# An expert loop rebuilt: biases from picked tables, second-layer weights in place, SiLU on ScalarE

## The reference

```python
xn = layernorm(x)
xm = xn * time_mix + shift(xn) * (1 - time_mix)
k = exp(min(xm @ Wk.T, 60)); v = xm @ Wv.T; r = xm @ Wr.T
# per channel, with a decay: wkv = sum_u W[t,u] k[u] v[u], sum_k = sum_u W[t,u] k[u] + 1e-16
s = (sigmoid(r) * wkv / sum_k) @ Wo.T
top1 = argmax(xn @ Wg + bg)                       # one of 8 experts for each token
y = relu(xn @ W1[top1] + b1[top1]) @ W2[top1] + b2[top1]      # 128 -> 512 -> 128
out = x + s * silu(y)
```

## Time and profile before

| | |
|---|---|
| median of 3 runs | 225.92 us |
| lowest of them | 225.53 us |
| the profiled execution's span | 224.6 us |
| PE busy | 193.5 us (86%) |
| DVE busy | 143.8 us (64%) |
| ACT busy | 123.2 us (55%) |
| POOL busy | 121.1 us (54%) |

### The profile page before, as it was taken

The page is one execution under the profiler, slowest core; times in us unless marked ns, Lnnn a source line. Parts: engine busy times, 40 slices in busy tenths (PEclk is TensorE's granted clock), DMA queues, the critical chain, the costliest instruction groups (busy, mean ns, idle before and its releaser), DMA issues.

```text
span 224.6 us, 4169 instructions
## 1 busy us (share of the span) xinstructions
PE 193.5 (86%) x1140; PEld 141.5 (63%) x1140; DVE 143.8 (64%) x335; ACT 123.2 (55%) x265; POOL 121.1 (54%) x196
## 2 busy tenths in 40 slices
PE   8829999995999999999999999999999999990000
PEld 3329996443447777787877877777777777770000
DVE  1599626799671278686876589666896668110792
ACT  2015555463489777767856578665787557640000
POOL 7055904472643576755875657755577556323250
PEclk9975555899799999999999999999999999997555
DMA  4939949200011111102111110111201122101994
GB/s 110 274 76 314 306 119 285 72 0 0 12 37 26 47 38 37 47 24 50 34 36 35 35 47 23 47 35 35 47 23 47 28 42 40 33 12 50 301 290 130
DMA packets 23818, 18.21 MB, mean 81 GB/s; under 512 B 3600, under 2 KB 20496, under 8 KB 23808
## 3 DMA queue, kind: packets, MB, share of 16 engines
q1 hardware_dynamic: 20560, 12.90, 20.2%
q0 software_dynamic: 2528, 5.18, 8.9%
q10 hardware_dynamic: 720, 0.01, 0.2%
HBM read 11.30 MB, written 6.75 MB: 80 GB/s over the span
## 4 chain that ended last, share of the span: by engine, by line
PE 75%; DVE 14%; DMA 6%; SPq 1%; issue 1%; DVEq 0%; ACT 0%; POOL 0%; POOLq 0%
PE ps L1001 20%; PE ps L1009 19%; PE ps L1000 11%; PE ps L921 6%; PE ps L952 4%; PE ps L1020 4%; PE ps L982 4%; PE ps L931 3%; DMA x_sb<-in_L_attn_x 3%; DVE ohlo L618 3%; DVE kT L759 3%; PE ps L1011 3%; DMA kT<-g_rows 2%; DVE stats L503 1%; DMA g_rows<-gout,si 1%; DVE kT L764 1%
## 5 line engine op out<-in xcount | busy, mean ns | idle before, releaser
L446 POOL DMA_INDIRECT g_rows<-gout,si x39 | 40.3, 1032 | 20.7 <-issue 13.9
L428 POOL DMA_INDIRECT xg<-xn_rows,gi x36 | 37.8, 1050 | 16.5 <-POOL si L436 9.0
L1009 PE MATMUL ps<-w2e,ohhi_hidif 128*128 128x128 f32 x312 | 45.2, 288 | 0.0
L650 DVE TENSOR_TENSOR gout<-ps,sgm 128x128 f32<-128x128 f32 x39 | 11.3, 289 | 50.3 <-ACT sgm L847 38.1
L1009 PEld LDWEIGHTS ps<-w2e,ohhi_hidif 128*128 128x128 f32 x312 | 37.7, 191 | 2.6
L841 ACT ACTIVATE ohhi_hidif<-ps 128x512 f32<-128x512 f32 x39 | 23.4, 599 | 29.1 <-remote 14.4
L1001 PE MATMUL ps<-xgT,w1e 128*128 128x128 f32 x156 | 38.1, 326 | 0.0
L1000 PE MATMUL ps<-xgT,w1e 128*128 128x128 f32 x156 | 30.2, 275 | 0.0
L1001 PEld LDWEIGHTS ps<-xgT,w1e 128*128 128x128 f32 x156 | 23.2, 188 | 6.7
L836 ACT COPY w2e<-w 128x512 f32 x39 | 24.1, 618 | 5.0 <-issue 4.7
L825 ACT COPY w1e<-w 128x512 f32 x39 | 24.1, 618 | 3.1 <-issue 0.5
(11 more groups left out here) (157 smaller groups left out, 304.6 us busy)
## 6 DMA issues: line engine op xcount, KB each, us to landing
x_sb<-in_L_attn_x SPq DMA_DIRECT2D x8, 256.0 KB, 6.9
w<-in_L_ffn_W SPq DMA_DIRECT2D x1, 2048.0 KB, 10.8
xn_rows<-xn_sb SPq DMA_DIRECT2D x2, 1024.0 KB, 6.7
kT<-g_rows SPq DMA_DIRECT2D x8, 256.0 KB, 5.0
out_x<-kT SPq DMA_DIRECT2D x8, 256.0 KB, 3.0
xg<-xn_rows,gi POOLq DMA_INDIRECT x40
g_rows<-gout,si POOLq DMA_INDIRECT x39, 2.3
wnat<-in_L_attn_Wk SPq DMA_DIRECT2D x1, 64.0 KB, 2.7
```

What stands on the lines that cost most here:

```text
L428: g.indirect_dma_start(xg[j][:, :], None, xn_rows, bass.IndirectOffsetOnAxis(gi[:, j:j + 1], 0)).then_inc(gathered[j], 16)
L446: g.indirect_dma_start(g_rows, bass.IndirectOffsetOnAxis(si[:, j:j + 1], 0), gout[j][:, :], None).then_inc(scattered[j], 16)
L1009: t.matmul(psYe[j % 2][:, 0:P], hidT[j % 2][:, cols], w2e[j % 2][:, cols], start=(c == 0), stop=False)
```

## The change

- **First-layer bias.** `b1` is loaded as 32 rows (expert, chunk) of 128, three times over, so that 96 rows hold the three bf16 parts (`bias_rows`). A table `pick1` holds, for each expert and chunk, 128 columns with ones in the three rows that belong to it. One matmul of 512 columns, at an address taken from a register, puts the whole bias into the PSUM bank, and the four weight products add to it. It replaces four bias products.
- **Second layer.** Its bias is one product of `ones` with `pick2`, at the register's address, and its weights are read in place in `w2`, at register addresses. The copy to `w2e` is gone. PE reads `etab` itself, once for each slot.
- **SiLU** is one operation of ACT, in place of the sigmoid there and a product on DVE. It waits for the scatter that frees `gout`.
- **The loop is written out** on every engine. POOL gathers and scatters with columns of `gidx` and `sidx`, not staged. PE waits before its first slot for all of k, v, r and for the tables.
- **The attention on DVE** stands by itself after the last block of k and v, no longer between the slots; `project` runs at slots 8, 12, ... 36 (`PROJECT_AFTER`, `PROJECT_EVERY`). The sigmoid of r is applied as r leaves PSUM, for all eight blocks on ACT. `kef` (exp(time_first) k + 1e-16) is computed on ACT for a whole batch behind each exp of k.
- **In the front**, POOL builds `same_row`, ACT copies it to `pick1` and computes the exponentials of the decays ahead of the first square root. The bias rows no longer go out of SBUF and back.

```diff
-        bias_nat = sb("bias_nat", [P, (E * HID + E * P) // P])
-        bias_r = sb("bias_r", [P, 2, (E * HID + E * P) // P])
-        bias_part = sb("bias_part", [P, 3, (E * HID + E * P) // P], BF16)
-        bias_mat = sb("bias_mat", [BR, HID + P], BF16)
+        bias_nat = sb("bias_nat", [BK, 2, P])
+        bias_r = sb("bias_r", [BK, 2, 2, P])
+        bias_part = sb("bias_part", [BK, 3, 2, P], BF16)
+        bias_rows = sb("bias_rows", [BK, 2, P], BF16)
+        same_row = sb("same_row", [P, BQ], BF16)
+        pick1 = sb("pick1", [BK, BQ, P], BF16)
+        pick2 = sb("pick2", [BK, E, P], BF16)
...
-            sp.dma_start(bias_nat[:, 0:E * HID // P],
-                         b1.rearrange("e h -> (e h)").rearrange("(p c) -> p c", p=P)).then_inc(ld_small, 16)
-            sp.dma_start(bias_nat[:, E * HID // P:],
-                         b2.rearrange("e h -> (e h)").rearrange("(p c) -> p c", p=P)).then_inc(ld_small, 16)
-            sp.wait_ge(ld_small, 16 * 7)
+            sp.wait_ge(bias_clear, 1)
+            for j in range(3):
+                sp.dma_start(bias_nat[j * BQ:(j + 1) * BQ, 0, :],
+                             b1.rearrange("e (c h) -> (e c) h", h=P)).then_inc(ld_bias, 16)
+                sp.dma_start(bias_nat[j * BQ:j * BQ + E, 1, :], b2).then_inc(ld_bias, 16)
+            sp.wait_ge(ld_small, 16 * 3)
             sp.wait_ge(ld_proj, 16 * 4)
+            sp.wait_ge(ld_bias, 16 * 6)
             sp.dma_start(w1[:, :, :], W1.rearrange("e d h -> d e h")).then_inc(ld_w1, 16)
             sp.dma_start(w2[:, :, :], W2.rearrange("e (c p) d -> p (e c) d", p=P)).then_inc(ld_w2, 16)
-
-            sp.wait_ge(bias_split, 1)
-            n1 = E * HID // P
-            for j in range(3):
-                rows = bias_mat[j * E:(j + 1) * E, :]
-                sp.dma_start(rows[:, 0:HID].rearrange("e (p c) -> e p c", c=n1),
-                             bias_part[:, j, 0:n1]).then_inc(bias_rows_in, 16)
-                sp.dma_start(rows[:, HID:].rearrange("e (p c) -> e p c", c=E),
-                             bias_part[:, j, n1:]).then_inc(bias_rows_in, 16)
...
+            step.link(g.memset(same_row[:, :], 0.0))
+            for m in range(0, P, BQ):
+                ins = g.affine_select(out=same_row[:, :], in_=same_row[:, :], compare_op=ALU.not_equal, fill=1.0,
+                                      base=-m, pattern=[[-1, BQ]], channel_multiplier=1)
+                if m + BQ < P:
+                    step.link(ins)
+            ins.then_inc(same_row_ready, 1)
+            g.memset(bias_nat[:, 1, :], 0.0).then_inc(bias_clear, 1)
...
+            for j in range(3):
+                rows = slice(j * BQ, (j + 1) * BQ)
+                ins = g.tensor_copy(bias_rows[rows, :, :], bias_part[rows, j, :, :])
+            step.link(ins)
+
+            g.tensor_tensor(pick2[:, :, :], bias_rows[:, 1, :].unsqueeze(1).to_broadcast([BK, E, P]),
+                            same_row[0:BK, 0:E].unsqueeze(2).to_broadcast([BK, E, P]), ALU.mult
+                            ).then_inc(bias_ready, 1)
...
+            def gather(s):
+
+                j = s % RING
+                if s >= RING:
+                    pool.wait_ge(xgT_ps, s - RING + 1)
...
+                                     bass.IndirectOffsetOnAxis(gidx[:, s:s + 1], 0)).then_inc(gathered[j], 16)
+
+            def scatter(s):
...
+            for s in range(RING):
+                gather(s)
+            pool.wait_ge(idx_ready, 1)
+            for s in range(SLOTS):
+                if s + RING < SLOTS:
+                    gather(s + RING)
+                if s >= 2:
+                    scatter(s - 2)
+            scatter(SLOTS - 2)
+            scatter(SLOTS - 1)
...
+                v.tensor_tensor(den[:, :], kef[:, here], zk[:, 0:BLK], ALU.add).then_inc(dve_step, 1)
...
-            gate_rows(TURNS - 1, LAST - 1, reused=True)
+            dve.wait_ge(kvr_out[2], NB)
+            for q in range(NB):
+                if q % NBB == 0:
+                    dve.wait_ge(k_ready, q // NBB + 1)
+                    dve.wait_ge(kef_ready, q // NBB + 1)
+                attend(q)
...
+            act.wait_ge(same_row_ready, 1)
+            s.copy(pick1[:, :, :], same_row[0:BK, :].unsqueeze(2).to_broadcast([BK, BQ, P])).then_inc(pick1_ready, 1)
...
+            act.wait_ge(ld_dec, 16 * 2)
+            s.activation(dec[:, :], tdec[:, :], ACT.Exp).then_inc(act_step, 1)
+            s.activation(ef[:, :], tfir[:, :], ACT.Exp).then_inc(act_step, 1)
+            act.wait_ge(act_step, 1)
+            s.activation(a_exp[:, :], dec[:, :], ACT.Exp, scale=-1.0).then_inc(dec_ready, 1)
             deviation(0)
...
+                act.wait_ge(kvr_ps[2], k + 1)
+                s.activation(rT[:, here], psY[:, :], ACT.Sigmoid).then_inc(kvr_out[2], 1)
...
+            for k in range(ACT_BLOCKS, NB):
+                act.wait_ge(kvr_ps[2], k + 1)
+                s.activation(rT[:, k * BLK:(k + 1) * BLK], psY[:, :], ACT.Sigmoid).then_inc(kvr_out[2], 1)
+
             def exp_k(b):
+                here = slice(b * T, (b + 1) * T)
                 act.wait_ge(k_capped, b + 1)
-                s.activation(kT[:, b * T:(b + 1) * T], kT[:, b * T:(b + 1) * T], ACT.Exp).then_inc(k_ready, 1)
+                s.activation(kT[:, here], kT[:, here], ACT.Exp).then_inc(k_ready, 1)
+                act.wait_ge(act_step, 2)
+                act.wait_ge(k_ready, b + 1)
+                s.activation(kef[:, here], kT[:, here], ACT.Copy, bias=K_EPS, scale=ef[:, 0:1]
+                             ).then_inc(kef_ready, 1)
...
+            def silu_y(n):
+
+                act.wait_ge(y_ps, n + 1)
+                if n >= RING:
+                    act.wait_ge(scattered[n % RING], 16 * (n // RING))
+                s.activation(gout[n % RING][:, :], psYe[n % 2][:, 0:P], ACT.Silu).then_inc(g_ready, 1)
...
+            copy_w1(0)
+            copy_w1(1)
             exp_k(0)
-            copy_w1(0, 1)
-            act.wait_ge(ld_w2, 16)
-            copy_w2(0, 0)
-            copy_xgT(0, 0)
+            copy_xgT(0)
             exp_k(1)
             act.wait_ge(inv_ps, 1)
-            turn(0, first=True)
-            act.wait_ge(kvr_out[2], NB)
             act.wait_ge(xn_stored, 16 * BATCH)
-            turn(1, attends=True)
-            with act.Fori(2, TURNS - 1) as i:
-                turn(i, attends=True, projects=True)
-            turn(TURNS - 1, last=True, projects=True)
-            sigmoid_y(TURNS - 1, LAST - 1)
+            for n in range(SLOTS):
+                if n + 1 < SLOTS:
+                    copy_xgT(n + 1)
+                relu(n)
+                if n + 2 < SLOTS:
+                    copy_w1(n + 2)
+                q, r = divmod(n - PROJECT_AFTER, PROJECT_EVERY)
+                if n >= PROJECT_AFTER and r == 1 and q < NB:
+                    copy_s(q)
+                if n:
+                    silu_y(n - 1)
+            silu_y(SLOTS - 1)
...
+            def layer1(n, e):
+
+                t.matmul(psH[n % 2][:, :], bias_rows[:, 0, :],
+                         pick1[:, bass.ds(e * HC, HC), :].rearrange("p c d -> p (c d)"), start=True, stop=False)
+                pe.wait_ge(layer1_in, n + 1)
+                pe.wait_ge(w1e_in, n + 1)
...
                     cols = slice(c * P, (c + 1) * P)
-                    weights = (w1e[j % 2][:, cols], xgT[j % 2][:, :])
-                    bias = (bias_mat[:, cols], sel_t[j][:, :])
-
-                    one, two = (bias, weights) if c % 2 == 0 else (weights, bias)
-                    t.matmul(psH[j % 2][:, cols], *one, start=True, stop=False)
-                    last = t.matmul(psH[j % 2][:, cols], *two, start=False, stop=True)
+                    last = t.matmul(psH[n % 2][:, cols], w1e[n % 2][:, cols], xgT[n % 2][:, :],
+                                    start=False, stop=c == HC - 1)
                 last.then_inc(hid_ps, 1)
...
+            def layer2(n, e):
+
+                if n >= 2:
+                    pe.wait_ge(g_ready, n - 1)
+                t.matmul(psYe[n % 2][:, 0:P], ones[0:BK, :],
+                         pick2[:, bass.ds(e, 1), :].rearrange("p o d -> p (o d)"), start=True, stop=False)
+                pe.wait_ge(hid_ready, n + 1)
                 for c in range(HC):
                     cols = slice(c * P, (c + 1) * P)
-                    t.matmul(psYe[j % 2][:, 0:P], hidT[j % 2][:, cols], w2e[j % 2][:, cols],
-                             start=(c == 0), stop=False)
-                t.matmul(psYe[j % 2][:, 0:P], sel_t[j][:, :], bias_mat[:, HID:],
-                         start=False, stop=True).then_inc(y_ps, 1)
+                    last = t.matmul(psYe[n % 2][:, 0:P], hidT[n % 2][:, cols],
+                                    w2[:, bass.ds(e * HC + c, 1), :].rearrange("p o d -> p (o d)"),
+                                    start=False, stop=c == HC - 1)
+                last.then_inc(y_ps, 1)
...
+            def expert(n):
+
+                return pe.value_load(etab[0:1, n:n + 1], min_val=0, max_val=E - 1)
```

(22 more changed lines are left out.)

342 lines of the change are left out of this document (80 added, 262 removed).

## The result

| | before | after |
|---|---|---|
| median, times beside each other | 226.34 us | 208.38 us (208.01 to 209.28) |
| ratio of the times | 1 | 0.9226, 95% interval [0.9188, 0.9264] |
| span of the profiled execution | 224.6 us | 206.6 us |
| PE busy | 193.5 us | 159.3 us |

The ratio compares fast runs alone: one of the four runs behind the 226.34 took 289.62 us and is not in it. Timed again, the changed kernel gave the same (0.9246 [0.919, 0.9301]); a third time it gave 0.9821 [0.9777, 0.9865], which the last experiments are about.

The account below looks back on a forecast made before the run. PE's slot beat was taken as the bound: 77.2 entry + (134.4 - 20.5) loop + 2.7 half clock = 193.8, plus a 22.2 tail = span 216.0; median 1.3 above, 217.3 us. Range: 211 less a little to 229.

Parts of the forecast that it names:

- the entry: Way into the expert loop: ACT's work after PE's last k, v, r product puts layer 1 of slot 1 at 77.2.
- the half clock: First stretch of the loop: PE at half clock until about 82.5, costing 2.7 us more, bounds nothing and 6.
- rival 2: Slot loop: POOL becomes the beat, held up by DVE; 3.2 against 3.0 us a slot, 8 more, 225; chance 0.13.
- the terms of the loop on PE: Slot on PE: layer 1 1.41, layer 2 1.15, transpose 0.21; 2.77 us, 0.54 less, 20.5 us over 38 slots.
- the port rule: POOL beside DVE: two-input or two-port DVE operations would shut POOL out and stretch it past PE's beat; forecast set it aside.
- Rival 1: PE between layer 2 and next transpose: register work not hidden, up to 1.0 us a slot, 256 us; chance 0.17.
- The tables in the r loop: ACT's r loop: a Sigmoid table load each turn, 1.28 us where PE has slack, counted as 0 to 0.7.
- The front: Before k, v, r: decays' exponentials precede ACT's first square root, which comes 0.65 us late, all passed on to PE.
- rival 4: Slot loop: PE's clock never comes back up; half clock throughout, some 110 us more, 325; chance 0.04.
- The tail: Behind PE's end: 22.5 us loses the gate product, 0.30, leaving 22.2.
- the eight projections: Projections on PE within the loop: each keeps its eight passes, 0.99 us at most, with no gain counted.

Follow-up runs that it names:

- the last experiments: Changed kernel unaltered, beside one without DVE's attention: 222.58 us, ratio 0.9821; changed kernel with turns 2 to 8 of ACT's slots looped again: 225.28 us.
- the flat kernel: Changed kernel with ACT's loop over the first six blocks of k, v, r written out: 203.08 us, ratio 0.8988; repeated, 203.34 us.
- again_tanh: Changed kernel with ACT's k, v, r loop written out, key scaling moved to DVE and the gate from a tanh; unaltered repeat: 198.89 us, ratio 0.8834.

## Why the prediction missed

**What bounds it: right for the kernel before, half right for the changed one.** PE's beat was the bound, the loop gains, the entry and the half clock take some back. But from about 103 us on it is POOL that sets the beat (rival 2). Direction and order of size held; the time was 9 us too high.

**The failed step: the terms of the loop on PE.** I took 1.09, 0.16, 0.99 and 0.21 us from rows of products that have neighbours of 24 rows, named them the cost of going between f32 and bf16, and carried them to products with neighbours of 96 rows. Measured are, in the same order, 0.89, 0.06, 0.94 and 0.11, and 0.22 for the one of 512 columns (forecast 0.32): 2.22 instead of 2.77, or 38 x 0.55 = 21 us less. With 64 rows the same kernel gives 2.76 and 217.03 us, so it was not the reading of the rows but the attribute that I chose: between these two kernels no type differs, only the rows. From the kernel before to the changed one the rows go from 24 to 96. The trace of before could not tell the two apart, since in it type and number of rows always changed together, and the range should have held that. The Trainium skill says (TensorEngine Tiling (Array Packing), Key Properties) that a change of tiling mode drains TensorE, and lists modes of 32, 64 and 128 rows (Available Configurations). The runs fit that, at 0.12 to 0.13 us a change, with 24 and 64 rows on one side and 96 on the other; that the products of 24 and 64 rows run in another mode is in no trace. I did not weigh it.

**Rival 2, POOL as the beat: it came, at another price.** I gave it 3.2 us a slot against 3.0. It is 2.56 at best and 2.84 by the means of its operations, against 2.22: it decides because PE became faster than I thought, and takes back part of the 21 us, as the profile lists 7.6 us of PE's waits for gathered rows behind 103 us. I had dropped the port rule since two rows differed by a tenth. Two rows can't bear out a mean: the same trace had 1.03 us over its 39 scatters and 1.05 over 36 of its gathers, with single ones at 1.44 and 1.74. In the changed kernel the mean of the 78 is 1.12, 0.13 more than without the attention. The Trainium skill (SBUF — State Buffer, Who interferes with whom) says that a DVE instruction with two SBUF inputs contends with a GpSimd instruction that reads SBUF, and that one with at most one such input, outside the two-port modes, does not; my wording had left out the condition on reading. The trace agrees: 1.26 us on the mean beside the first kind, never over 1.00 otherwise.

**Rival 1, register work on PE: didn't happen.** No idle time of PE's free slots is charged to issue; the slot is the sum of its products (0.22 + 0.89 + 0.06 + 0.94 + 0.11 = 2.22). The work itself is in the trace, 0.30 for the load, 0.15 for the check and 0.05 to 0.06 for each of six addresses, together about 0.8 a slot where I had 1.0.

**The entry: 77.2 forecast, 79.1 measured, the rest of two larger errors.** The steps behind the last kvr product (w1 twice, one load, exp, scaling, twice) came as written: 11.5 us from the sigmoid to the second xgT, forecast 11.3. The sigmoid came at 67.4 instead of 65.7. The tables in the r loop, which I had at 0 to 0.7, made it 4.6 later (62.74 in the flat kernel): I counted one load a turn beside slack on PE, and there are two, which make ACT the bound of that stage. Against that the sigmoid of the flat kernel is 3.0 earlier than my 65.7. The front was not 0.65 late but early: tfir landed 5.9 us after its issue instead of the 7.8 that I took from before, the first root came at 10.73 instead of the 12.85 forecast, and the first key product at 34.52 instead of 36.20 in the kernel before.

**The clock: right.** Half clock until 83.8 in the loop, 4.7 us at half, so 2.4 lost (2.7 forecast). Then it stayed up, against rival 4.

**The tail:** 22.2 forecast, 21.6 measured. The gate product is gone as forecast; the first load of rows landed in 3.1 us instead of 4.2, which I had not in the sum.

**Sum.** PE's end was forecast at 193.8 and came at 185.0: + 1.9 for the entry, - 0.3 for the clock, - 20.9 for the slots, - 0.3 for the eight projections (0.90 more than a free slot each, 0.94 before), and + 10.8 for what the slots take beyond that. Of the 10.8 the profile lists 7.6 as waits for gathered rows, and by the starts such a wait costs more than is listed (0.82 against 0.65, above); how the remainder divides was not worked out.

## What to carry to other kernels

Before a duration is carried from one instruction to another, list every attribute that the rows change together (type, rows, columns, neighbours), and see which of them the diff changes: what can't be told apart belongs into the range. On TensorE, zero-padding a small bias product to over 64 rows took 0.96 us off a slot of 3.31 with no other change. A function with a table of its own inside a repeating loop on ScalarE, beside copies, cost two loads a turn here, and one load in all with the loop written out. When one engine gains a third of its beat, work out the next engine's again at the new beat, from the mean of its operations and not from two of them. A shorter beat also takes away the time in which late operations of other engines went unnoticed.

## What the hardware showed that I had not expected

- Products of 24 or 64 rows among products of 128 rows cost 0.12 to 0.13 us at each change from one to the other; with 96 rows no more than 0.05 a step is left (slots of 3.32, 3.32 and 2.35 us, and 2.76 and 2.22).
- No drain behind a table load: with 12 loads in the r loop the next operation started 1.29 us after the load's start (42.13 to 43.42). The Trainium skill (ScalarE: Activation LUTs, What ACT_TABLE_LOAD costs) states 1.38 us more; the runs don't show it.
- Tanh and Exp needed no load between them: none lies between the last tanh (65.77) and the exponential (68.20) of again_tanh.
- Beside DVE operations with two inputs in SBUF, POOL's indirect transfers take 1.26 us on the mean and up to 2.02; beside reciprocals, with one, or beside nothing they take 0.96 to 1.00.
- The same kernel took 208.2 to 208.4 us in two sets and 222.6 in a third, with ACT's stops and the clock's drops, while the medians of the kernel before stayed within 225.6 to 226.5 in all. The change's gain is 7.5 to 7.7% in the one case and 1.8% in the other.
